# Layer 1's gathers moved into layer 2's first stage, which adds, normalises, turns and projects by quarters

## The chip, the cores and the metric

One Trainium2 chip, one core of it. The metric is the device time of one launch in microseconds, the median of the runs shown. A core has five engines that run side by side: TensorE (PE, matmuls and transposes), VectorE (DVE), ScalarE (ACT), GpSimd (POOL) and SyncE (SP, which here only issues DMAs). Each runs its own instructions strictly in the order in which they are written; they wait for one another on semaphores.

## The reference, cut to what matters

Four layers, each an attention-like part and a feed-forward part around a residual `x` of 2048 tokens by 128 features in float32. The change lies between layer 1's feed-forward part (each token goes through one of 64 experts) and the projections that open layer 2's attention-like part:

```
# layer 1, feed-forward: every token by the matrix of its own expert
sel = argmax(softmax(xt @ gate_w.T + gate_b), -1);  order = argsort(sel)
ys  = ragged_dot(xt[order], expert_w, counts) + expert_b[sel[order]]
x   = x + gb * (ys put back into the order of the tokens)
# layer 2, attention: norm over the features, then three projections
h = layernorm(x) * (1 + ca) + sa
R, K, V = h @ Wr.T, h @ Wk.T, h @ Wv.T
# then a scan over the tokens on R, K, V (leaky cells that fire at 1), and from it attn_out
x1 = layernorm(h + attn_out @ Wo.T)
```

## The kernel before, in words

Tokens are held as 16 tiles of 128 (`NT = 16`), four tiles to a quarter (`NC4 = 4` quarters of 512 tokens). A stage opens a `Block`, in which each engine has its own list; at the end of a block all engines meet before the next one begins, and at the end of a part of a layer they meet through a somewhat longer clean-up. What SP is told outside a block (the loads of a layer part) it issues when it gets there, while other engines may already be in the next block.

Layer 1's experts (`stage_l1_experts`): POOL scatters the normalised tokens by 16 indirect DMAs into a table in DRAM, sorted by expert in groups of 64 (L1856). SP reads it back in six loads (L1843), PE turns and multiplies (L1891, L1907), DVE multiplies by the gate into `y` (L1938), SP stores `y` in six pieces into a second table `sorted_out` (L1849). POOL waits for all six stores, then gathers each token's row back by 16 indirect DMAs into `back` (L1860), four to a quarter. For each quarter DVE waits for its four gathers, adds `back` to the residual `g.x` (L1945) and takes the statistics of its four tiles with `bn_stats` (L139). There the layer part ends.

Layer 2 (`layer2_spiking`) first has SP load its weights (L89: `l2_wrkvo`, `l2_ln1cols` and nine more, then L209), and ACT wait for `l2_ln1cols`. Then `stage_l2_mix`:

- DVE: `norm.start` (16 `bn_aggr`, L239, variance, L241; ACT's root, L419; reciprocal and one correction step, L243 to L248), `norm.normalise` of all 16 tiles (L403), then every second copy of projections out of PSUM (L2152), a fill with 0.9 (L2154), and the scan `lif` (L2049, L2050, then L2037 and L2040 in turn, 32 steps), on DVE alone.
- PE: six idle products to keep busy (L376), transposes of a quarter (L411), the three projections of a quarter (L2113, twelve in all), turning one quarter ahead of the one it projects.
- ACT: the root, for each quarter scale and shift out of PSUM into `hT` (L423), and the other half of the copies (L2131).
- POOL: waits for all 16 normalised tiles, then `RowsFinish` (six small operations in a chain, L225 to L231, which finish layer 2's rows of gates and scales), then two operations over all 2048 tokens that make `h_tm` (L2138 and L2141), needed only after the scan.

Two things are the same before and after: the order of DVE's scan, and everything after it.

Of the kernel before, what the change touches and what calls it, by code (L numbers as in the profile page):

```python
# [23 lines left out]
P = 128  # L24
# [354 lines left out]
class Norm:  # L379
# [1422 lines left out]
def stage_l1_experts(nc, d, g, loads, W, sorted_in, sorted_out, zeroed, weights_loaded, slot, member, gang_expert):  # L1802
# [6 lines left out]
    with Stage(nc, "l1exp") as st:  # L1809
        ident16 = loads["ident16"]  # L1810
# [4 lines left out]
        back = st.sb("back", [P, NT, P])  # L1815
# [17 lines left out]
        gathered = [st.sem(f"gathered{j}") for j in range(NC4)]  # L1833
        chain = st.sem("chain")
        with st.block() as block:

            @block.sync
            def _(sp):
                sp.wait_ge(scattered, 16 * NT)
                n = pairs // LOADS  # L1840
                for i in range(LOADS):
                    src = sorted_in[i * n * P:(i + 1) * n * P, :]
                    sp.dma_start(rows[:, i * n:(i + 1) * n, :], src.rearrange("(k p) f -> p k f", p=P))\  # L1843
                      .then_inc(rows_loaded[i], 16)
                for i in range(STORES):
                    sp.wait_ge(y_gated, QUADS // STORES * (i + 1))
                    m = GANGS // STORES
                    dst = sorted_out[i * m * GANG:(i + 1) * m * GANG, :]
                    sp.dma_start(dst.rearrange("(k p) f -> p k f", p=GANG), y[:, i * m:(i + 1) * m, :])\  # L1849
                      .then_inc(y_stored, 16)  # L1850

            @block.gpsimd
            def _(pool):
                pool.wait_ge(zeroed, 17)
                for t in range(NT):
                    pool.indirect_dma_start(out=sorted_in, out_offset=bass.IndirectOffsetOnAxis(  # L1856
                        ap=slot[:, t:t + 1], axis=0), in_=g.xn[:, t, :], in_offset=None).then_inc(scattered, 16)
                pool.wait_ge(y_stored, 16 * STORES)
                for t in range(NT):
                    pool.indirect_dma_start(out=back[:, t, :], out_offset=None, in_=sorted_out,  # L1860
                                            in_offset=bass.IndirectOffsetOnAxis(ap=slot[:, t:t + 1], axis=0))\
                        .then_inc(gathered[t // 4], 16)
                for j in range(NC4):
                    pool.wait_ge(gathered[j], 16 * 4)
# [62 lines left out]
            def _(dve):  # L1927
# [12 lines left out]
                link = Chain(dve, chain)  # L1940
                dve.wait_ge(bias_added, NC4)
                for j in range(NC4):
                    dve.wait_ge(gathered[j], 16 * 4)
                    ts = slice(4 * j, 4 * j + 4)
                    link(dve.tensor_tensor(g.x[:, ts, :], g.x[:, ts, :], back[:, ts, :], ALU.add))  # L1945
                    tile_stats(dve, g, g.x, range(4 * j, 4 * j + 4))


def layer1_experts(nc, d, g):
    sorted_in = nc.dram_tensor("l1_sorted_in", [GANGS * GANG, P], F32, kind="Internal").ap()  # L1950
    sorted_out = nc.dram_tensor("l1_sorted_out", [GANGS * GANG, P], F32, kind="Internal").ap()
# [124 lines left out]
def stage_l2_mix(nc, loads, g, h_tm, r):  # L2076

    with Stage(nc, "l2mix") as st:
        norm = adaln_norm(st, g, 2, SCALE_A, SHIFT_A)
        rows_finish = RowsFinish(st, 2)  # L2080
        g.rows_finished.add(2)
# [13 lines left out]
        out_done = st.sem("out_done")  # L2095
        chain = st.sem("chain")
        with st.block() as block:  # L2097

            @block.tensor
            def _(pe):  # L2100
                pe.wait_ge(loads.done, loads.all)
                norm.turn(pe, 0, ps_t[:, 0, :])
                for n in range(3 * NC4):
                    j, i = n // 3, n % 3
                    if i == 0:
                        if j + 1 < NC4:
                            if j >= 1:
                                norm.turned(pe, j - 1)
# [13 lines left out]
            def _(act):  # L2122
                norm.root(act)
                norm.scale(act, 0, ps_t[:, 0, :])
# [10 lines left out]
            def _(pool):  # L2135
                pool.wait_ge(norm.tile_normed, NT)
                rows_finish(pool, g)
# [8 lines left out]
            def _(dve):  # L2146
                link = Chain(dve, chain)
                norm.start(dve)
                norm.normalise(dve, range(NT))
                for n in range(1, 3 * NC4, 2):  # L2150
                    dve.wait_ge(in_done, n + 1)
                    dve.tensor_scalar(tokens_of(X_steps, LENGTH, n % 3, n // 3), by_chunk(ps[:, n % 6, :], LENGTH),  # L2152
                                      0.5, None, ALU.mult).then_inc(copied[1], 1)
# [1354 lines left out]
def program(nc, d, out, stages=None):  # L3508

    with ExitStack() as ctx:  # L3510
# [11 lines left out]
        g.stats = sb("stats", [P, NT, 6])  # L3522
        g.silu = sb("silu", [P, 4])
# [123 lines left out]
```

## Time and profile before

| | us |
|---|---|
| median of 3 runs | 1733.46 (1730.65 to 1736.72) |
| the profiled execution, its own time | 1726.0 |
| its span in the trace | 1724.2 |
| DVE busy over the span | 1303.6 (76%) |
| PE busy over the span | 1239.0 (72%) |
| last `y` gated to first gather started | 1016.06 to 1021.67 |
| 16 gathers, first start to last start | 1021.67 to 1040.50 |
| last add of layer 1 begins | 1042.99 |
| first instruction of DVE in layer 2 begins | 1045.63 |
| first scan instruction of DVE begins | 1066.68 |

Times with a decimal point and four digits before it are positions in the span of the profiled execution. The rows further down come from four views of it: the list of waits (which engine sat idle before which instruction, and what released it), the timeline (instructions in order of time, neighbours of one kind merged), the tile view (one buffer), and the table of stretches (busy time of each engine, granted clock of TensorE as a share of 2.4 GHz, and DMA). A matmul on float32 data is two passes in the trace and is counted x2.

### The profile page before, as it was taken

What the parts mean: (1) busy time and instruction counts of PE and PEld (TensorE: products, weight loads), DVE (VectorE), ACT (ScalarE), POOL (GpSimd) and SP (SyncE); (2) the same over time, 40 slices, a digit from 0 to 9 for tenths busy, and PEclk for the clock granted to TensorE, in tenths of its full rate; (3) what the DMA queues carried; (4) which work ended last, traced back from release to release, by engine and by line L of the source; (5) the groups of instructions that cost most, each with busy time, mean ns of one, the idle gap of its engine ahead of it and who ended that gap; (6) DMA issues with size and microseconds to landing.
All of it is one profiled execution on the core that took longest, in us unless ns stands there. A gap on an engine that the chain in (4) does not pass through costs nothing. (4 is left out here: it accounts for less than half of the span.)

```text
span 1724.2 us, 29793 instructions
## 1 busy us (share of the span) xinstructions
PE 1239.0 (72%) x10670; PEld 619.8 (36%) x10674; DVE 1303.6 (76%) x3511; ACT 889.7 (52%) x1757; POOL 236.1 (14%) x275
## 2 busy tenths in 40 slices
PE   7799999999999997574993453060215989824686
PEld 3122222222222223354982342040113547623445
DVE  6999999999999972447237236989897568578873
ACT  4099999999999996412521122020002775502553
POOL 2000000000000000003410324030003321000223
PEclk9599999999999999667995586565656988965668
DMA  2100000011000000000004331000001721031001
GB/s 73 37 14 27 21 21 21 22 28 28 23 21 20 21 2 2 15 29 1 1 1 188 101 84 46 0 0 1 1 0 27 228 68 43 4 116 49 22 22 31
DMA packets 45030, 62.88 MB, mean 36 GB/s; under 512 B 12785, under 2 KB 34356, under 8 KB 44484
## 3 DMA queue, kind: packets, MB, share of 16 engines
q1 hardware_dynamic: 38243, 49.71, 9.7%
q0 software_dynamic: 5440, 10.67, 2.3%
q8 instruction: 85, 1.39, 0.3%
q10 hardware_dynamic: 1200, 0.59, 0.1%
q14 instruction: 62, 0.51, 0.1%
HBM read 34.10 MB, written 13.63 MB: 28 GB/s over the span
## 5 line engine op out<-in xcount | busy, mean ns | idle before, releaser
L842 ACT ACTIVATE l0att_probs<-l0att_ps_sv 128x512 f32<-128x512 f32 x960 | 521.2, 596 | 80.0 <-PE l0att_ps_sv L811 68.1
L888 DVE TENSOR_REDUCE l0att_half_negmax<-l0att_ps_m 128x1 f32<-128x1024 f32 x480 | 547.1, 1216 | 5.6 <-PE l0att_ps_m L741 5.6
L773 PE MATMUL l0att_ps_sv<-l0att_probs,l_V_aug 128*32 128x256 f32 x4096 | 325.3, 392 | 4.8 <-ACT l0att_pv_sb L833 4.7
L811 PE MATMUL l0att_ps_sv<-l_Q,l_K 51*128 51x512 bf16 x992 | 194.5, 388 | 4.0 <-ACT l0att_probs L850 2.4
L741 PE MATMUL l0att_ps_m<-l_K,l_Q 48*128 48x512 bf16 x960 | 185.9, 384 | 11.1 <-DVE l0att_half_negmax L888 7.1
L773 PEld LDWEIGHTS l0att_ps_sv<-l0att_probs,l_V_aug 128*32 128x32 f32 x4096 | 83.0, 108 | 197.4 <-issue 100.9
L811 PEld LDWEIGHTS l0att_ps_sv<-l_Q,l_K 51*128 51x128 bf16 x992 | 48.0, 92 | 207.4 <-ACT l0att_probs L842 188.1
L472 POOL CAST l0att_nm<-l0att_negmax 128x16 bf16<-128x16 f32 x16 | 3.2, 198 | 515.0 <-DVE l0att_negmax L864 515.0
L2862 ACT ACTIVATE l3loc_probs<-l3loc_ps_s 128x320 f32<-128x320 f32 x128 | 48.9, 435 | 36.0 <-PE l3loc_ps_s L2839 35.3
L2040 DVE SCALAR_TENSOR_TENSOR l2spk_lif_v<-l2spk_U 128x64 f32<-128x64 f32 (+1 forms) x368 | 60.8, 207 | 0.0
L741 PEld LDWEIGHTS l0att_ps_m<-l_K,l_Q 48*128 48x128 bf16 x960 | 47.1, 95 | 28.5 <-DVE l0att_half_negmax L888 19.0
L2890 DVE TENSOR_REDUCE l3loc_negmax<-l3loc_ps_m 128x2 f32<-128x320 f32 x128 | 53.5, 484 | 3.8 <-PE l3loc_ps_m L2795 3.8
L2305 PE MATMUL l2spk_ps<-l_X,l2spk_w_terms 128*128 128x512 bf16 x48 | 11.8, 411 | 61.3 <-DVE l_X L2335 61.3
L2117 PE MATMUL l2mix_ps<-l_mix_l_wrkvo,l2mix_X 128*128 128x128 f32 x32 | 8.3, 441 | 65.4 <-DVE l2mix_X L2177 65.4
L3285 ACT ACTIVATE l3exp_passed<-l3f_experts_l_places,l3exp_neg_rank 128x257 bf16<-128x257 f32 x112 | 46.0, 500 | 0.0
L1938 DVE TENSOR_TENSOR l1exp_y<-l1exp_ps_y,mod_rows 64x512 f32<-64x512 f32 x24 | 16.4, 683 | 36.3 <-PE l1exp_ps_y L1907 36.3
L1562 DVE TENSOR_TENSOR l1chunk_T<-l1chunk_T,l1chunk_ps_t 128x512 f32<-128x512 f32 x20 | 13.8, 688 | 36.0 <-PE l1chunk_ps_t L1463 36.0
L2223 ACT ACTIVATE l2hid_half_b<-l_hidden_l_b 128x4 f32<-128x4 f32 x1 | 0.2, 205 | 75.5 <-PEq L2097 75.5
L2325 ACT ACTIVATE l2spk_U<-l2spk_ps,l2spk_half_b 128x512 f32<-128x512 f32 x2 | 2.3, 1127 | 70.8 <-PE l2spk_ps L2305 70.7
L1517 POOL TENSOR_TENSOR l1chunk_C<-l1chunk_A,l_chunks_masks 128x2048 f32<-128x2048 f32 x7 | 31.7, 4534 | 47.3 <-DVE l1chunk_A L1549 25.9
L2037 DVE SCALAR_TENSOR_TENSOR l2spk_U<-l2spk_lif_v,l_X 128x64 f32<-128x64 f32 x212 | 37.5, 219 | 0.4 <-DVE l2spk_lif_mid L2055 0.4
L3243 PE MATMUL l3exp_ps_c<-l3exp_part,l3exp_ones 128*128 128x15 bf16 x56 | 10.7, 191 | 36.1 <-DVE l3exp_part L3392 36.0
(736 smaller groups left out, 2391.8 us busy)
## 6 DMA issues: line engine op xcount, KB each, us to landing
l_K<-l_kp SPq DMA_DIRECT2D x192, 32.0 KB
l_Q<-l_qp SPq DMA_DIRECT2D x192, 32.0 KB
l1ffn_W<-in_l_expert_w_dram SPq DMA_DIRECT2D x1, 4096.0 KB
l3f_experts_l_w<-in_l_w_dram SPq DMA_DIRECT2D x2, 2048.0 KB
l_sorted_in<-l1ffn_zeros SPq DMA_DIRECT2D x1, 3072.0 KB
l1exp_rows<-l_sorted_in SPq DMA_DIRECT2D x6, 512.0 KB, 5.6
l_sorted_out<-l1exp_y SPq DMA_DIRECT2D x6, 512.0 KB, 4.6
l_Q<-in_local_mask_q_dram POOLq DMA_DIRECT2D x2, 1170.0 KB, 17.3
```

Source lines behind the costliest of these rows:

```text
L741: mm = pe.matmul(dst[:, i * BANK:(i + 1) * BANK], Q[at, h % HEAD_BUFS, c1(t)], K[at, h % HEAD_BUFS, c4(2 * half + i)], start=True, stop=True)
L773: mm = pe.matmul(ps_v[32 * c:32 * c + 32, cols], V_aug[:, kt, h, :], probs[:, kt % 2, c, cols], start=(kt == 0 and part == 0), stop=(kt == ...
L811: pe.matmul(dst, K[at, h % HEAD_BUFS, c1(kt)], Q[at, h % HEAD_BUFS, c4(2 * pair + i)], start=True, stop=True).then_inc(last_scored[i] if l ...
L842: act.activation(probs[:, kt % 2, c, :], ps_s[:, n % 3, :], ACT.Exp).then_inc(expd, 1)
L888: dve.tensor_reduce(half_negmax[:, h % 2, t, half:half + 1], src, AX_X, ALU.max, negate=True).then_inc(m_read, 1)
L1517: pool.tensor_tensor(C[:, l % 2, :, :], A[:], mask(l, NT), ALU.mult).then_inc(c_ready, 1)
L1938: dve.tensor_tensor(y[:, 4 * n:4 * n + 4, :], ps_y[0:GANG, n % 4, :].rearrange("p (k f) -> p k f", k=4), gates, ALU.mult).then_inc(y_gated, 1)
L2037: link.mark(dve.scalar_tensor_tensor(U[:, t, half], before[:, half], 0.5, X[:, t, half], ALU.mult, ALU.add))
L2040: link.mark(dve.scalar_tensor_tensor(v[:, half], U[:, t, half], 1.0, U[:, t, half], ALU.is_lt, ALU.mult))
L2862: act.activation(probs[:, n % 3, 2 * half:2 * half + 2, :].rearrange("p h c -> p (h c)"), ps_s[:, u % SCORE_BUFS, 0:2 * SPAN], ACT.Exp).th ...
L2890: dve.tensor_reduce(negmax[:, 2 * half:2 * half + 2, t], heads2(src[:, 0:2 * SPAN]), AX_X, ALU.max, negate=True).then_inc(m_read, 1)
L3285: ins = act.activation(passed[:, e % 2, t, :], place_row[:], ACT.Sign, bias=neg_rank[:, e, t:t + 1])
```

## The change

The 16 gathers leave layer 1's last stage and open layer 2's first stage on POOL; SP waits for the six stores before layer 1's stage ends. `RowsFinish` of layer 2 moves from POOL's list in layer 2 to POOL's list in layer 1, behind the scatters. The index tile `slot` is kept over both layers. DVE's add and statistics move to layer 2, and everything that it does up to the projections' copies is done one quarter at a time, with the copies that are its own between the quarters. PE no longer turns one quarter ahead, and runs twelve idle products ahead of the turns of quarters 1 to 3. ACT takes the root by quarters.

```
     # class Norm
+    def start_quarter(self, dve, link, j):
+        ts = slice(4 * j, 4 * j + 4)
+        mv, var, std, rstd, corr = (buf[:, ts] for buf in (self.mv, self.var, self.std, self.rstd, self.corr))
+        for t in range(4 * j, 4 * j + 4):
+            link.mark(dve.bn_stats(self.g.stats[:, t, :], self.src[:, t, :]))
+        link.wait()
+        for t in range(4 * j, 4 * j + 4):
+            link.mark(dve.bn_aggr(self.mv[:, t, :], self.g.stats[:, t, :]))
+        link.wait()
+        dve.tensor_scalar(var, mv[:, :, 1], LN_EPS, None, ALU.add).then_inc(self.var_ready, 1)
+        dve.wait_ge(self.std_ready, j + 1)
+        link(dve.reciprocal(rstd, std))
+        link(dve.tensor_tensor(corr, rstd, rstd, ALU.mult))
+        link(dve.tensor_tensor(corr, corr, var, ALU.mult))
+        link(dve.tensor_scalar(corr, corr, -0.5, 1.5, ALU.mult, ALU.add))
+        link(dve.tensor_tensor(rstd, rstd, corr, ALU.mult))
+    def root_quarter(self, act, j):
+        ts = slice(4 * j, 4 * j + 4)
+        act.wait_ge(self.var_ready, j + 1)
+        act.activation(self.std[:, ts], self.var[:, ts], ACT.Sqrt).then_inc(self.std_ready, 1)
...
     # stage_l1_experts, SP, POOL, DVE
+                sp.wait_ge(y_stored, 16 * STORES)
...
-                pool.wait_ge(y_stored, 16 * STORES)
-                for t in range(NT):
-                    pool.indirect_dma_start(out=back[:, t, :], out_offset=None, in_=sorted_out, ...)\
-                        .then_inc(gathered[t // 4], 16)
-                for j in range(NC4):
-                    pool.wait_ge(gathered[j], 16 * 4)
+                pool.wait_ge(scattered, 16 * NT)
+                rows_finish(pool, g)
...
-                for j in range(NC4):
-                    dve.wait_ge(gathered[j], 16 * 4)
-                    ts = slice(4 * j, 4 * j + 4)
-                    link(dve.tensor_tensor(g.x[:, ts, :], g.x[:, ts, :], back[:, ts, :], ALU.add))
-                    tile_stats(dve, g, g.x, range(4 * j, 4 * j + 4))
...
     # stage_l2_mix, PE
-                norm.turn(pe, 0, ps_t[:, 0, :])
...
                     if i == 0:
-                        if j + 1 < NC4:
-                            if j >= 1:
-                                norm.turned(pe, j - 1)
-                            norm.turn(pe, j + 1, ps_t[:, (j + 1) % 2, :])
+                        if j >= 1:
+                            keep_busy(pe, g, ps_t[:, j % 2, :], 12)
+                        norm.turn(pe, j, ps_t[:, j % 2, :])
                         norm.turned(pe, j)
...
     # stage_l2_mix, ACT
-                    if i == 0 and j + 1 < NC4:
-                        norm.scale(act, j + 1, ps_t[:, (j + 1) % 2, :])
+                    if i == 0:
+                        norm.root_quarter(act, j)
+                        norm.scale(act, j, ps_t[:, j % 2, :])
...
     # stage_l2_mix, POOL
+                for t in range(NT):
+                    pool.indirect_dma_start(out=back[:, t, :], out_offset=None, in_=g.sorted_out, ...)\
+                        .then_inc(gathered[t // 4], 16)
                 pool.wait_ge(norm.tile_normed, NT)
-                rows_finish(pool, g)
...
     # stage_l2_mix, DVE
-                norm.start(dve)
-                norm.normalise(dve, range(NT))
-                for n in range(1, 3 * NC4, 2):
-                    dve.wait_ge(in_done, n + 1)
-                    dve.tensor_scalar(tokens_of(X_steps, LENGTH, n % 3, n // 3), ..., 0.5, None, ALU.mult)...
+                for j in range(NC4):
+                    ts = slice(4 * j, 4 * j + 4)
+                    dve.wait_ge(gathered[j], 16 * 4)
+                    link(dve.tensor_tensor(g.x[:, ts, :], g.x[:, ts, :], back[:, ts, :], ALU.add))
+                    norm.start_quarter(dve, link, j)
+                    norm.normalise(dve, range(4 * j, 4 * j + 4))
+                    for n in range(3 * j, 3 * j + 3):
+                        if n % 2 == 1:
+                            dve.wait_ge(in_done, n + 1)
+                            dve.tensor_scalar(tokens_of(X_steps, LENGTH, n % 3, j), ..., 0.5, None, ALU.mult)...
```

## Rows read from the trace of the kernel before

**Rows 1.** Waits, 1008 to 1085: who waited for what, total us, times, longest.

```profile
POOL l1exp_back L1860 <- DMA l_sorted_out<-l1exp_y: 46.8, 1, 46.8
DVE x_res L1945 <- DMA l1exp_back<-l_sorted_out,l1ffn_slot: 21.3, 4, 11.3
DVE l2mix_X L2152 <- PE l2mix_ps L2113: 5.3, 6, 1.1
DVE l2mix_norm_rstd L243 <- ACT l2mix_norm_std L419: 1.9, 1, 1.9
```

**Rows 2.** Timeline, end of layer 1: start us, us, engine, line, op.

```profile
1016.06 0.68 DVE L1938 TENSOR_TENSOR l1exp_y<-l1exp_ps_y,mod_rows 64x512 f32<-64x512 f32 x1 [0.19 <-PE l1exp_ps_y L1907]
1021.67 0.99 POOL L1860 DMA_INDIRECT l1exp_back<-l_sorted_out,l1ffn_slot  x1 [46.79 <-DMA l_sorted_out<-l1exp_y]
1028.08 0.69 DVE L1945 TENSOR_TENSOR x_res<-x_res,l1exp_back 128x512 f32<-128x512 f32 x1 [11.33 <-DMA l1exp_back<-l_sorted_out,l1ffn_slot]
1028.81 0.87 DVE L139 BATCH_NORM_STATS2 stats<-x_res 128x6 f32<-128x128 f32 x4
...
1040.50 0.94 POOL L1860 DMA_INDIRECT l1exp_back<-l_sorted_out,l1ffn_slot  x1 [0.31 <-issue]
...
1043.71 0.87 DVE L139 BATCH_NORM_STATS2 stats<-x_res 128x6 f32<-128x128 f32 x4
```

**Rows 3.** Timeline, from layer 2's first instruction to the scan.

```profile
1045.63 1.17 DVE L239 BATCH_NORM_AGGREGATE l2mix_norm_mv<-stats 128x2 f32<-128x6 f32 x16 [1.05 <-PEq L3532]
...
1048.36 2.93 PE L376 MATMUL l2mix_ps_t<-ident_sb 128*128 128x128 f32 x12 [32.34 <-DMA l_mix_l_wrkvo<-in_l_wrkvo_dram]
...
1050.06 4.19 DVE L403 TENSOR_SCALAR xn<-x_res,l2mix_norm_mv,l2mix_norm_rstd 128x128 f32<-128x128 f32 x16
...
1054.34 0.87 POOL L225 TENSOR_SCALAR mod_rows<-mod_rows 128x256 f32<-128x256 f32 x1 [12.90 <-DVE xn L403]
...
1059.85 4.54 POOL L2138 TENSOR_TENSOR l_h_tm<-xn,mod_rows 128x2048 f32<-128x2048 f32 x1
...
1064.47 4.50 POOL L2141 TENSOR_TENSOR l_h_tm<-l_h_tm,mod_rows 128x2048 f32<-128x2048 f32 x1
1064.78 1.03 DVE L2152 TENSOR_SCALAR l2mix_X<-l2mix_ps 128x512 f32<-128x512 f32 x1 [0.67 <-PE l2mix_ps L2113]
...
1066.68 2.58 DVE L2037 SCALAR_TENSOR_TENSOR l2mix_U<-l2mix_lif_shifted,l2mix_X 128x96 f32<-128x96 f32 x2
1069.18 0.42 DVE L2040 SCALAR_TENSOR_TENSOR l2mix_lif_v<-l2mix_U 128x96 f32<-128x96 f32 x2
```

**Rows 4.** Timeline, start of the experts' stage: the first indirect DMA of a block.

```profile
954.03 0.28 DVE L1930 TENSOR_TENSOR l1exp_gated_table<-l1ffn_bias_l_expert_b,mod_rows 64x128 f32<-64x128 f32 x1 [0.38 <-PEq L1744]
954.74 1.13 POOL L1856 DMA_INDIRECT l_sorted_in<-xn,l1ffn_slot  x1 [13.81 <-POOLq L1744]
```

**Rows 5.** Timeline, layer 2's next stage, the same norm and first projections.

```profile
1141.66 0.17 DVE L241 TENSOR_SCALAR l2hid_norm_var<-l2hid_norm_mv 128x16 f32<-128x16 f32 x1
...
1143.25 4.19 DVE L403 TENSOR_SCALAR l_h_tm<-l_x_tm,l2hid_norm_mv,l2hid_norm_rstd 128x128 f32<-128x128 f32 x16
...
1145.76 3.70 PE L2218 MATMUL l2hid_ps<-hT,l_hidden_l_w1T 128*128 128x512 f32 x8
...
1147.87 1.11 DVE L2244 TENSOR_SCALAR l_X<-l2hid_ps,l2hid_half_b 128x512 f32<-128x512 f32 x1 [0.42 <-PE l2hid_ps L2218]
```

**Rows 6.** Stretches: us, busy (instructions) of PE, PEld, DVE, ACT, POOL; clock, DMA share, GB/s.

```profile
1018.00:1020.00 2.00, 0.00 (x0) 0.00 (x0) 0.00 (x0) 0.00 (x0) 0.00 (x0) 0.87 0.82 175
1050.00:1052.00 2.00, 2.00 (x12) 2.00 (x11) 1.96 (x9) 0.00 (x0) 0.00 (x0) 0.50 0.81 203
...
1053.00:1054.00 1.00, 0.99 (x2) 0.68 (x3) 1.00 (x5) 0.78 (x1) 0.00 (x0) 0.69 0.42 166
1054.00:1055.00 1.00, 1.00 (x3) 0.40 (x3) 0.25 (x1) 0.54 (x1) 0.66 (x1) 1.00 0.00 0
```

**Rows 7.** Stretches in layer 3's experts, same columns: TensorE about 70% busy with gaps.

```profile
1610.00:1612.00 2.00, 1.64 (x13) 1.23 (x13) 1.65 (x9) 1.06 (x3) 0.00 (x0) 1.00 0.00 0
...
1614.00:1616.00 2.00, 1.72 (x10) 1.57 (x9) 1.77 (x10) 0.18 (x1) 1.20 (x2) 0.50 0.33 90
```

**Rows 8.** Tile views of layer 1's gathers and, below, layer 3's: 16 each.

```profile
DMA to landing us min/median/max: 2.4/2.5/2.7
...
DMA to landing us min/median/max: 2.2/2.8/3.7
```

More of the change, by code:

```diff
@@ L1809, in stage_l1_experts @@
     with Stage(nc, "l1exp") as st:
+        rows_finish = RowsFinish(st, 2)
+        g.rows_finished.add(2)
         ident16 = loads["ident16"]
@@ L1814, in stage_l1_experts @@
         y = st.sb("y", [GANG, GANGS, P])
-        back = st.sb("back", [P, NT, P])
         chosen = st.sb("chosen", [EXPERTS, S])
@@ L1832, in stage_l1_experts @@
         y_stored = st.sem("y_stored")
-        gathered = [st.sem(f"gathered{j}") for j in range(NC4)]
-        chain = st.sem("chain")
         with st.block() as block:
@@ L1857, in _ @@
                         ap=slot[:, t:t + 1], axis=0), in_=g.xn[:, t, :], in_offset=None).then_inc(scattered, 16)
-                pool.wait_ge(y_stored, 16 * STORES)
-                for t in range(NT):
-                    pool.indirect_dma_start(out=back[:, t, :], out_offset=None, in_=sorted_out,
-                                            in_offset=bass.IndirectOffsetOnAxis(ap=slot[:, t:t + 1], axis=0))\
-                        .then_inc(gathered[t // 4], 16)
-                for j in range(NC4):
-                    pool.wait_ge(gathered[j], 16 * 4)
+                pool.wait_ge(scattered, 16 * NT)
+                rows_finish(pool, g)
             @block.tensor
@@ L1939, in _ @@
                         "p (k f) -> p k f", k=4), gates, ALU.mult).then_inc(y_gated, 1)
-                link = Chain(dve, chain)
                 dve.wait_ge(bias_added, NC4)
-                for j in range(NC4):
-                    dve.wait_ge(gathered[j], 16 * 4)
-                    ts = slice(4 * j, 4 * j + 4)
-                    link(dve.tensor_tensor(g.x[:, ts, :], g.x[:, ts, :], back[:, ts, :], ALU.add))
-                    tile_stats(dve, g, g.x, range(4 * j, 4 * j + 4))
 def layer1_experts(nc, d, g):
@@ L1951, in layer1_experts @@
     sorted_out = nc.dram_tensor("l1_sorted_out", [GANGS * GANG, P], F32, kind="Internal").ap()
+    slot = g.slot
+    g.sorted_out = sorted_out
     ZEROS = 8
@@ L1955, in layer1_experts @@
         zeros = st.sb("zeros", [P, ZEROS * P])
-        slot = st.sb("slot", [P, NT], I32)
         idx = st.sb("idx", [P, NT, 8], U32)
@@ L2079, in stage_l2_mix @@
         norm = adaln_norm(st, g, 2, SCALE_A, SHIFT_A)
-        rows_finish = RowsFinish(st, 2)
-        g.rows_finished.add(2)
         w = loads["l2_wrkvo"]
@@ L2095, in stage_l2_mix @@
         out_done = st.sem("out_done")
+        back = st.sb("back", [P, NT, P])
+        gathered = [st.sem(f"gathered{j}") for j in range(NC4)]
         chain = st.sem("chain")
@@ L2122, in _ @@
             def _(act):
-                norm.root(act)
-                norm.scale(act, 0, ps_t[:, 0, :])
                 for n in range(3 * NC4):
                     j, i = n // 3, n % 3
-                    if i == 0 and j + 1 < NC4:
-                        norm.scale(act, j + 1, ps_t[:, (j + 1) % 2, :])
+                    if i == 0:
+                        norm.root_quarter(act, j)
+                        norm.scale(act, j, ps_t[:, j % 2, :])
                     if n % 2 == 0:
@@ L2135, in _ @@
             def _(pool):
+                for t in range(NT):
+                    pool.indirect_dma_start(out=back[:, t, :], out_offset=None, in_=g.sorted_out,
+                                            in_offset=bass.IndirectOffsetOnAxis(ap=g.slot[:, t:t + 1], axis=0))\
+                        .then_inc(gathered[t // 4], 16)
                 pool.wait_ge(norm.tile_normed, NT)
-                rows_finish(pool, g)
                 pool.tensor_tensor(h_tm[:], g.xn[:], bcast(mod_row(g, 2, SCALE_A).unsqueeze(1), P, NT, P),
@@ L2147, in _ @@
                 link = Chain(dve, chain)
-                norm.start(dve)
-                norm.normalise(dve, range(NT))
-                for n in range(1, 3 * NC4, 2):
-                    dve.wait_ge(in_done, n + 1)
-                    dve.tensor_scalar(tokens_of(X_steps, LENGTH, n % 3, n // 3), by_chunk(ps[:, n % 6, :], LENGTH),
-                                      0.5, None, ALU.mult).then_inc(copied[1], 1)
+                for j in range(NC4):
[7 more added lines that the diff above has]
+                            dve.wait_ge(in_done, n + 1)
+                            dve.tensor_scalar(tokens_of(X_steps, LENGTH, n % 3, j), by_chunk(ps[:, n % 6, :], LENGTH),
+                                              0.5, None, ALU.mult).then_inc(copied[1], 1)
                 link.mark(dve.memset(decay[:], 0.9))
@@ L3522, in program @@
         g.stats = sb("stats", [P, NT, 6])
+        g.slot = sb("slot", [P, NT], I32)
         g.silu = sb("silu", [P, 4])
```

## Prediction

> **What bounds the kernel now.** I read the waits around the change first, then the timeline. In the waits [rows 1] the reader is to see that between layer 1's last product and layer 2's scan nobody computes much: DVE sits 21.3 us before its four adds, waiting for gathers. The timeline [rows 2] gives the order: last `y` gated at 1016.06, the stores landed at the latest at 1021.67, when POOL begins, and then 16 gathers at one per (1040.50 - 1021.67) / 15 = 1.255 us, so a quarter each 5.02 us. From then on the path is: last gather, add and statistics, change of stage (1044.58 to 1045.63, 1.05 us), norm, 16 normalised tiles (1050.06 to 1054.25), twelve projections, copies until 1065.81, scan [rows 3]. The scan is on DVE alone and everything behind it is unchanged, so the question is when it gets going.
>
> That moment isn't 1066.68, where its first instruction starts. The first pair takes 2.58 us where the next takes 0.42, and it ends at 1069.26, just behind POOL's second `h_tm` operation, which ends at 1068.97 [rows 3]. DVE's copies out of PSUM beside the same operation took their normal 1.03. So the scan's first instruction, which reads two tensors of SBUF, stood still until POOL was through. I therefore count from the end of POOL: 1068.97 before.
>
> The Trainium skill (SBUF — State Buffer, section "SBUF: two separate sides") says that VectorE and GpSimd share one pair of ports, that it is an exclusive lock for a whole instruction, and that a VectorE instruction with two SBUF inputs needs it against a GpSimd instruction that reads SBUF. By this rule the start of the scan follows POOL's end after the change too; the trace's 2.58 against 0.42 us agrees.
>
> **What the change does, part by part.** Call A the start of the first add (1028.08 before) and T the end of the last normalised tile (1054.25 before).
>
> *The gathers' start.* It now lies behind a change of layer part. The stores still land by 1021.67, then 1.05 us as at 1044.58 to 1045.63 [rows 2, 3]; the first indirect DMA of a block starts 0.71 us behind DVE's first instruction there and takes 1.13 instead of 0.95 [rows 4]. Sum 1.9; the landing may be some 0.2 earlier than 1021.67, so I take 1.7. The ends are 1.05 (no start-up) and 1.9. Besides, SP now issues layer 2's twelve loads in the same microseconds as the first gathers; before they filled 0.81 of the DMA engines at 203 GB/s with nobody in need of them but PE and ACT [rows 6]. The trace has no gather under such a load; the nearest are layer 3's, 2.2 to 3.7 us to landing against 2.4 to 2.7 here [rows 8]. Ends 0 and 1.2, I take 0.8, since most of the load stands in the first quarter's way. A = 1028.08 + 2.5 = 1030.6.
>
> *A quarter's front on DVE.* Add and statistics 1.60 (1028.08 to 1029.68) [rows 2]. Four aggregates: 16 take 1.17, at about 0.07 apart and 0.15 the last, so 0.35 plus 0.05 of waits [rows 3]. Variance, ACT's root, reciprocal and correction: 1141.66 to 1143.25, 1.59, which hardly depends on width since these are a chain of short operations with waits [rows 5]; the narrower 4 columns could save 0.1 in all. Four normalised tiles: 16 in 4.19, so 1.11. Sum 4.7. Before, the norm's chain was paid once for 16 tiles; now four times, 3 x 1.59 = 4.8 us more of DVE. The 1.9 us in which DVE waited for ACT, held by the load of `l2_ln1cols` [rows 1], goes: that load now lands before A.
>
> *A quarter's back.* This is the heart of it. DVE's copy of quarter j stands in its list ahead of the add of quarter j+1, and waits for PE, which waits for ACT, which waits for PE's turns of that very quarter. Queued behind the waiting copy: the next quarter's add, and through it everything. What that costs is in the next stage, which has the same turns and projections: fourth tile normalised at 1143.25 + 1.11 = 1144.36, first projection at 1145.76, DVE's copy of the second at 1147.87, so 3.51 from tile to copy [rows 5]. With 1.05 of the copy [rows 3] and a wait, 4.6 us for quarters 0 and 2, which have one copy of DVE (n = 1, 7). Quarters 1 and 3 have two (n = 3, 5 and 9, 11); the later one waits for one projection more. Eight passes take 3.70, a projection 0.86 to 0.92: 3.51 + 0.86 + 1.05 = 5.45.
>
> So a quarter occupies DVE for 9.3 or 10.15 us, twice the 5.02 at which quarters land: from quarter 1 on the gathers are hidden and DVE's chain is the bound. T = A + 4 x 4.7 + 4.6 + 5.45 + 4.6 = A + 33.45, at TensorE's upper clock.
>
> *The clock.* The granted clock was 0.50 when the stage began, and 1.00 from 1054 on, after TensorE had worked without a pause since 1048.36; it fell to 0.50 within 4 us of TensorE's last work at the end of layer 1 [rows 3, 6]. In the changed stage the six idle products run as soon as `l2_wrkvo` is there (2.73 us after the stage begins, as at 1045.63 to 1048.36, so about 1025.4, to 1028.3), TensorE then idles until the turns at about 1034, and quarter 0's first two projections run at 1.2 GHz: 2 x 0.86 = 1.7 more. Then projections and twelve idle products run without a break, which should raise it. Later quarters have TensorE about 65% busy in pieces; in layer 3 at such a share the clock was 1.00 in one stretch and 0.50 two stretches on [rows 7]. A later single-copy quarter at the lower level costs 1.7, a double-copy one 2.6; what quarter 3 loses is behind T, hidden by POOL (below). Ends 0 and 4.3 for quarters 1 and 2; I take 1.0, since twelve idle products stand just ahead. The idle products themselves (24 passes, 2.6 us; at the lower clock 5.9 by the 2.93 for 12 [rows 3]) lie beside DVE's copy and front, 4.9 us up to the next quarter's first tile; at the upper clock they cost nothing, at the lower one up to 2.3 a quarter.
>
> T = 1030.6 + 33.45 + 1.7 + 1.0 = 1066.75.
>
> *POOL.* `RowsFinish` (1054.34 to 1059.85, 5.5 us [rows 3]) goes from between T and `h_tm` to the time behind the scatters, when POOL has nothing to do and DVE waits for the first product: free. POOL then needs 4.54 + 4.50 + 0.2 = 9.2 behind T. DVE's last copies end at T + 5.45, fills at T + 6.3, so the scan again stands until POOL's end, T + 9.2 = 1075.95. Against 1068.97: **+7.0 us**. Moving `RowsFinish` away gives 5.5 us of this path back; without it the sum would be +12.5.
>
> *Further places.* SP's wait for the stores replaces POOL's and adds nothing. The index tile and the semaphores cost nothing on the path. Behind the scan all is as before.
>
> The profiled execution's own time was 1726.0 (span 1724.2); with +7.0 it is 1733.0. The median of the runs lies 7.5 above it, so I forecast 1733.46 + 7.0 = 1740.5.
>
> **Rivals.**
>
> 1. *Less: TensorE is at the upper clock soon and the gathers start early.* A = 1029.1 (only the 1.05), no cold quarter: T = 1062.6, POOL's end 1071.8, +2.8; or POOL does not hold the scan, then the first pair ends at about T + 6.7, also near +4. For it: the low ends of each term, and the idle products. Against it: TensorE's pause of about 6 us (1028.3 to 1034.5) ahead of quarter 0. Time about 1736.5, within 0.3%.
>
> 2. *More: each quarter begins at the lower clock.* 1.7 + 2.6 + 1.7 instead of 2.7, and the idle products, twice as long, delay the turns of two quarters by 1 to 2 us: +10.5 to +14. For it: the alternation in layer 3 [rows 7], and before each quarter's turns TensorE has paused 1.5 to 2.5 us. Against it: projections and idle products make over 5 us in a row. Time about 1745.
>
> 3. *Faster: the quarters do overlap.* If DVE's wait for its copies is short enough that a quarter takes no more than the 5.02 us at which it lands, the last quarter's add is ready at 1042.99 + 2.5, T = 1050.2, and POOL's end 1059.4: -9.6, 1724. It decides where DVE's period per quarter falls under 5 us; break-even (T = 1059.8) is a period of (1059.8 - 1030.6 - 4.7) / 3 = 8.2 us. Against it: front and back as measured add to 9.3 and 10.15, and DVE's list has no way around the copy. Only if both parts are a fifth shorter than in these rows does it begin to gain.
>
> 4. *It does what it says but the time is elsewhere*: the sum rests on POOL and DVE at one place; nothing in the trace suggests another path there.
>
> **How the numbers follow.** About 0.3% (5.2 us) is what a measurement of this kernel can tell from no change. Forecast +5.2 to +10: chance 0.42. Rival 1 (0 to +5.2): 0.30. Rival 2 (beyond +10): 0.18. Rival 3 and other gains: 0.10, of which 0.02 is a gain under 0.3%. Slower: 0.42 + 0.18 = 0.60; same: 0.32; faster: 0.08. The range leaves out the gains and the far end of rival 2: from -1 to +15, 1732.5 to 1748.5. The likeliest case's own range is 1738.5 to 1743.5.
>
> **What would show it.** Right: DVE's adds about 9.5 to 12 us apart, with waits of about 2.5 us for `l2mix_ps` before each quarter's first copy of DVE, and no wait for gathers after the first; first add at 1030 to 1031; the scan's first pair again ending with POOL's second `h_tm` operation, near 1076; clock 0.50 in quarter 0. Wrong: adds 5 us apart (rival 3); the first pair of the scan at 0.42 us; gathers waited for more than once; a clock at 0.50 throughout (rival 2) or never after 1035 (rival 1).

## The result, and the profile after

| | median us | runs | ratio to before, 95% interval |
|---|---|---|---|
| before | 1729.90 | 20 | |
| after | 1737.45 | 20 | 1.0047 [1.0035, 1.0060] |

The change makes the kernel slower by 7.55 us. The forecast was 1740.5: 3 us too high, because it started from the median of three runs, 1733.46, where that of all twenty is 1729.90; the step of +7.0 that it put on top was right. In the profiled executions the span went from 1724.2 to 1734.0.

The span is a poor measure of the place: with nothing changed there, layer 3's local attention began 13.6 us later in the second trace and the last step of its expert search 10.5, while the scan had ended 6.9 later. I use one inside the trace, called **D** below: from the end of the last gated `y` of layer 1 to the end of the scan's first pair on DVE. Before it is 1069.26 - 1016.74 = 52.5 [rows 2, 3]; after, 1076.60 - 1017.01 = 59.6. The difference is +7.1 us; forecast were +7.0, and the medians differ by 7.55.

The changed kernel from the last gated `y` to the scan (timeline, DVE's and POOL's lines that answer to [rows 2, 3]):

```profile
1016.33 0.68 DVE L1955 TENSOR_TENSOR l1exp_y<-l1exp_ps_y,mod_rows 64x512 f32<-64x512 f32 x1 [0.19 <-PE l1exp_ps_y L1924]
...
1023.52 1.08 POOL L2146 DMA_INDIRECT l2mix_back<-l_sorted_out,slot  x1 [41.04 <-POOLq L3550]
...
1027.45 0.95 POOL L2146 DMA_INDIRECT l2mix_back<-l_sorted_out,slot  x1 [0.30 <-issue]
...
1031.41 0.69 DVE L2163 TENSOR_TENSOR x_res<-x_res,l2mix_back 128x512 f32<-128x512 f32 x1 [14.40 <-DMA l2mix_back<-l_sorted_out,slot]
...
1034.91 1.12 DVE L425 TENSOR_SCALAR xn<-x_res,l2mix_norm_mv,l2mix_norm_rstd 128x128 f32<-128x128 f32 x4
...
1041.37 1.02 DVE L2169 TENSOR_SCALAR l2mix_X<-l2mix_ps 128x512 f32<-128x512 f32 x1 [5.34 <-PE l2mix_ps L2123]
1042.24 0.67 DVE L2163 TENSOR_TENSOR x_res<-x_res,l2mix_back 128x512 f32<-128x512 f32 x1
1042.43 1.29 POOL L2146 DMA_INDIRECT l2mix_back<-l_sorted_out,slot  x1 [0.30 <-issue]
...
1049.25 1.03 DVE L2169 TENSOR_SCALAR l2mix_X<-l2mix_ps 128x512 f32<-128x512 f32 x1 [2.42 <-PE l2mix_ps L2123]
...
1051.86 0.67 DVE L2163 TENSOR_TENSOR x_res<-x_res,l2mix_back 128x512 f32<-128x512 f32 x1
...
1061.67 1.03 DVE L2169 TENSOR_SCALAR l2mix_X<-l2mix_ps 128x512 f32<-128x512 f32 x1 [5.22 <-PE l2mix_ps L2123]
1062.54 0.67 DVE L2163 TENSOR_TENSOR x_res<-x_res,l2mix_back 128x512 f32<-128x512 f32 x1
...
1066.02 1.12 DVE L425 TENSOR_SCALAR xn<-x_res,l2mix_norm_mv,l2mix_norm_rstd 128x128 f32<-128x128 f32 x4
...
1071.82 4.50 POOL L2153 TENSOR_TENSOR l_h_tm<-l_h_tm,mod_rows 128x2048 f32<-128x2048 f32 x1
...
1073.17 3.43 DVE L2049 SCALAR_TENSOR_TENSOR l2mix_U<-l2mix_lif_shifted,l2mix_X 128x96 f32<-128x96 f32 x2
```

The reader is to see three things. The adds (L2163) begin at 1031.41, 1042.24, 1051.86 and 1062.54, so 10.8, 9.6 and 10.7 us apart, while POOL issues a quarter's gathers in 5.0. Only the first add waits for a gather; what precedes each later one is a copy (L2169) that waited for PE. And the scan's first pair ends with POOL's second `h_tm` operation, as before [rows 3]. The waits of this stretch say the same in two lines: DVE's wait for gathers fell from 21.3 us in four to 14.4 in one, its wait for projections rose from 5.3 to 16.7 [rows 1].

```profile
DVE l2mix_X L2169 <- PE l2mix_ps L2123: 16.7, 6, 5.3
DVE x_res L2163 <- DMA l2mix_back<-l_sorted_out,slot: 14.4, 1, 14.4
```

TensorE's clock in the same trace, in the columns of [rows 6], one stretch ahead of quarter 0 and one in each quarter's projections or their start:

```profile
1029.00:1031.00 2.00, 0.00 (x0) 0.00 (x0) 0.00 (x0) 0.00 (x0) 1.59 (x2) 0.96 0.85 224
...
1036.00:1038.00 2.00, 1.13 (x4) 0.73 (x4) 0.03 (x1) 0.78 (x1) 1.50 (x2) 0.50 0.23 55
1048.00:1050.00 2.00, 1.92 (x5) 0.96 (x6) 0.75 (x1) 0.03 (x1) 0.00 (x0) 1.00 0.00 0
1058.00:1060.00 2.00, 2.00 (x3) 0.97 (x4) 0.00 (x0) 0.04 (x1) 0.00 (x0) 0.50 0.00 0
1068.00:1070.00 2.00, 1.61 (x4) 0.87 (x5) 0.45 (x1) 0.33 (x1) 2.00 (x1) 1.00 0.00 0
```

Quarters 0 and 2 projected at 0.50 (1.2 GHz), 1 and 3 at 1.00 (2.4 GHz). DVE waited 5.34 and 5.22 us for its first copy in the former and 2.42 in the latter. Only part of that is the clock: in quarters 0 and 2 DVE's first copy is of the quarter's second projection, in 1 and 3 of its first. At the upper clock the wait in quarters 0 and 2 is 3.31 and 3.27 (e5 below), so the clock's share is 2.0 us each.

### The profile page after: what moved, and what is told of

Read it like the earlier page. It is cut to its first block and busy times, and to the rows that moved or that the text cites. A ratio compares the mean times of both kernels' runs of the same rounds, so it can differ in the third digit from the quotient of the medians.

```text
span 1734.0 us, 29959 instructions
## 1 busy us (share of the span) xinstructions
PE 1260.9 (73%) x10746; PEld 630.2 (36%) x10746; DVE 1307.4 (75%) x3529; ACT 891.1 (51%) x1760; POOL 235.8 (14%) x275
## 5 line engine op out<-in xcount | busy, mean ns | idle before, releaser
L3260 PE MATMUL l3exp_ps_c<-l3exp_part,l3exp_ones 128*128 128x15 bf16 x56 | 10.7, 191 | 37.7 <-DVE l3exp_part L3409 37.6
```

## The experiments

All twelve, with D and what the theory gave for it. Ratios are to the kernel before, on the same chip in the same hour. Each difference of D from the kernel before lies inside the interval of its ratio, so D stands for what the whole kernel gains or loses, as far as the intervals can tell.

| | D forecast | D measured | ratio, 95% interval |
|---|---|---|---|
| before | | 52.5 | 1 |
| after | | 59.6 | 1.0047 [1.0035, 1.0060] |
| e1 gathers moved, nothing by quarters | 49.6 | 50.0 | 0.9995 [0.9977, 1.0013] |
| e2 before, `RowsFinish` early | 50.4 | 50.7 | 0.9986 [0.9973, 0.9999] |
| e3 copies one quarter later, no idle products | 46.7 | 46.3 | 0.9978 [0.9963, 0.9994] |
| e4 `h_tm` by quarters | 56.6 | 61.2 | 1.0047 [1.0030, 1.0064] |
| e5 more idle products | 56.2 | 57.3 | 1.0018 [1.0006, 1.0029] |
| e6 other loads late | 58.2 | 59.4 | 1.0029 [1.0016, 1.0042] |
| e7 = e3 and e4 | 45.4 | 46.9 | 0.9972 [0.9959, 0.9985] |
| e8 = e3 and e6 | 44.9 | 44.0 | 0.9949 [0.9934, 0.9964] |
| e9 `RowsFinish` back in layer 2 | 65.1 | 60.6 (65.2, see there) | 1.0070 [1.0046, 1.0094] |
| e10 no idle products | 62.2 | 62.2 | 1.0060 [1.0037, 1.0082] |
| e11 = e3 with idle products | 49.7 | 48.8 | 0.9977 [0.9960, 0.9993] |
| e12 the changed kernel again | 57 to 62 | 58.9 | 1.0056 [1.0036, 1.0075] |

**e1: is it the move or the quarters?** Against the changed kernel:

```
-                    norm.start_quarter(dve, link, j)
-                    norm.normalise(dve, range(4 * j, 4 * j + 4))
-                    for n in range(3 * j, 3 * j + 3): ...copies
+                    for t in range(4 * j, 4 * j + 4): ...bn_stats
+                norm.start(dve); norm.normalise(dve, range(NT)); copies
     # and TensorE and ScalarE as in the kernel before
```

> The changed kernel with the gathers, the adds and RowsFinish where the change puts them, but with the norm, the turns, the projections and the copies again as before: all four adds first, then one norm over 16 tiles, TensorE turning one quarter ahead, no idle products ahead of quarters 1 to 3. Measure: from the end of the last gated y of layer 1 to the end of the scan's first pair, 52.5 us in the kernel before (1016.74 to 1069.26), 59.6 in the changed one (1017.01 to 1076.60). Theory (the loss is VectorE's list, in which a quarter's copies stand ahead of the next quarter's add): the adds come every 5 us, the last about 28 us behind the last gated y, the norm's last tile at 36.7, RowsFinish is out of the way, the pair ends at about 49.6: 2.9 us less than before and 10 less than the changed kernel. Rival (the loss is the gathers' later start and their company by the loads, and the quartering is neutral): about 59, as the changed kernel.

Timeline of DVE and POOL, the last add to the scan:

```profile
1043.85 0.69 DVE L2166 TENSOR_TENSOR x_res<-x_res,l2mix_back 128x512 f32<-128x512 f32 x1 [3.33 <-DMA l2mix_back<-l_sorted_out,slot]
1048.27 4.19 DVE L425 TENSOR_SCALAR xn<-x_res,l2mix_norm_mv,l2mix_norm_rstd 128x128 f32<-128x128 f32 x16
...
1057.15 4.54 POOL L2156 TENSOR_TENSOR l_h_tm<-l_h_tm,mod_rows 128x2048 f32<-128x2048 f32 x1
...
1065.47 0.43 DVE L2049 SCALAR_TENSOR_TENSOR l2mix_U<-l2mix_lif_shifted,l2mix_X 128x96 f32<-128x96 f32 x2
```

The last add begins 27.9 us behind the last gated `y` instead of 45.5; D is 50.0, 9.6 less than in the changed kernel with the same gathers at the same place. So the move costs nothing, and the quarters cost all of it. The gathers do come later: the last add begins 27.9 us behind the last gated `y` where it was 26.3 before. But the change of stage, 1.05 us, no longer stands behind it, and DVE's wait for ACT's root fell from 1.92 to 0.28. Against the kernel before D is 2.5 less, and most of that is `RowsFinish`, which is early in e1 as well: e2, which has nothing but that, comes to 50.7. The ratio, 0.05% down with 0.18% either way, holds this gain and no change too.

**e2: what holds the scan.** In the kernel before, `rows_finish` goes from POOL's list in layer 2 to just behind the scatters.

> The kernel before with RowsFinish alone moved behind the scatters. Measure as in the first experiment (52.5 us before). Theory (POOL's h_tm holds the scan's first pair): POOL's second operation ends at about 1063.5, before the scan starts at 1066.7, the pair takes 0.42 instead of 2.58 us, and the measure is 50.4, 2.1 us less. Rival (the first pair is slow in itself, or held by something else): the pair still takes 2.6 us and the measure stays at 52.5.

```profile
1060.08 4.54 POOL L2142 TENSOR_TENSOR l_h_tm<-l_h_tm,mod_rows 128x2048 f32<-128x2048 f32 x1
...
1067.49 0.43 DVE L2041 SCALAR_TENSOR_TENSOR l2mix_U<-l2mix_lif_shifted,l2mix_X 128x96 f32<-128x96 f32 x2
```

POOL ends at 1064.62, the pair begins at 1067.49 and takes 0.43. With POOL out of the way the same instruction isn't slow. That piece of the change is a gain by itself, 1.8 us in D, and its interval lies below 1, if barely.

**e3 and e11: the order on DVE.**

```
                     norm.normalise(dve, range(4 * j, 4 * j + 4))
-                    for n in range(3 * j, 3 * j + 3): ...copies of quarter j
+                    if j >= 1:
+                        copies(j - 1)
+                copies(NC4 - 1)
     # ScalarE: root of quarter j + 1 right behind the scale of quarter j
     # TensorE, in e3 alone:
-                        if j >= 1:
-                            keep_busy(pe, g, ps_t[:, j % 2, :], 12)
```

> The changed kernel with VectorE's copies of quarter j written behind the add and norm of quarter j+1, ScalarE's root of quarter j+1 ahead of its copies of quarter j, and no idle products ahead of quarters 1 to 3. Measure as in the first experiment (59.6 us in the changed kernel). Theory (VectorE's wait for its copies is the loss): adds 4.7 to 7 us apart instead of 9.6 to 10.8, last normalised tile about 37 us behind the last gated y, measure 46.7: 13 less than the changed kernel, 6 less than before. Rival (the period is the engines' work, not the order, with ScalarE or TensorE the next bound): adds 8 us or more apart, measure 55 or more.

> The third experiment with the twelve idle products left ahead of quarters 1 to 3: VectorE's copies one quarter later, ScalarE's root earlier, nothing else against the changed kernel. Measure as in the first experiment (46.3 us in the third, 59.6 in the changed kernel). Theory: the order of the copies alone is worth nearly all of it; with VectorE no longer waiting, the idle products, 2.84 us each time, now stand ahead of turns that are ready: TensorE becomes the bound at about 7.5 us a quarter, measure 49.7, 3.4 more than the third, 9.9 less than the changed kernel. Rival (the gain of the third came from leaving the idle products out): near 59.

The scan's first pair in e3, then DVE's waits of e3 and of e11, from the last gated `y` to the scan:

```profile
1060.07 3.44 DVE L2049 SCALAR_TENSOR_TENSOR l2mix_U<-l2mix_lif_shifted,l2mix_X 128x96 f32<-128x96 f32 x2
```

```profile
DVE l2mix_X L2164 <- PE l2mix_ps L2121: 2.9, 3, 1.5
```

```profile
DVE l2mix_X L2166 <- PE l2mix_ps L2123: 6.2, 3, 4.8
DVE l2mix_norm_rstd L412 <- ACT l2mix_norm_std L421: 3.8, 4, 2.6
```

The wait for projections is 2.9 us where it was 16.7; D fell by 13.3. With the idle products left in (e11) it still fell by 10.8: four fifths of the gain is order alone, that of DVE's list together with ACT's earlier root. The other 2.5 us are those products, which here stand ahead of turns that are ready. On the whole kernel e3 and e11 can't be told apart.

**e4 and e7: `h_tm` by quarters.** POOL's two operations over 16 tiles become eight over four, each pair behind its own quarter's normalised tiles.

> The changed kernel with POOL's two h_tm operations done quarter by quarter as the quarters are normalised, instead of over all 16 tiles at the end. Measure as in the first experiment (59.6 us in the changed kernel). Theory (the scan is held only until POOL is through): POOL ends about 2.4 us behind the last normalised tile, the first pair takes 0.42 instead of 3.43 us, measure 56.6, 3.0 less. Rival (POOL's operations now stand in the way of VectorE's add and normalise of the next quarter, up to 1.15 us each): 1.8 less or nothing.

> The third and fourth experiment together: VectorE's copies one quarter later, and h_tm by quarters on POOL. Measure as in the first experiment (46.3 in the third, in which the scan's first pair took 3.44 us). The fourth showed that POOL's smaller operations hold single operations of VectorE's front for 0.6 to 0.7 us each, 1.3 in the second quarter. Theory: the pair takes 0.43, saving 3.0, and the fronts of quarters 2 and 3 lose 1.3 and 0.8: measure 45.4. Rival (the fronts, now without pauses between them, lose more, or TensorE's clock falls): 47 or more.

Both missed. The scan's pair did take 0.43 in both. But the small operations stood in the way of the fronts, and in e4 the clock fell as well. Of e4, one held operation of quarter 1's front and the clock in that quarter's projections:

```profile
1044.65 0.79 DVE L410 TENSOR_SCALAR l2mix_norm_var<-l2mix_norm_mv 128x4 f32<-128x4 f32 x1
```

```profile
1050.00:1052.00 2.00, 2.00 (x3) 0.96 (x4) 0.00 (x0) 0.00 (x0) 1.26 (x1) 0.50 0.00 0
```

The holds cost e4 only 1.3 us (this operation, and one of 0.16 that took 0.84). The larger part of its miss is the clock: quarter 1's projections took 5.27 us instead of 2.84, and with the holds the adds on either side of them lie 13.5 us apart instead of 9.6; quarter 3's took 4.35 instead of 2.84, with POOL no longer there to hide it. Both quarters ran at 1.00 in the changed kernel. Timeline of e7, POOL's and DVE's lines of quarter 2:

```profile
1048.08 1.37 DVE L413 TENSOR_TENSOR l2mix_norm_corr<-l2mix_norm_rstd 128x4 f32<-128x4 f32 x1
1048.13 1.28 POOL L2152 TENSOR_TENSOR l_h_tm<-xn,mod_rows 128x512 f32<-128x512 f32 x1
...
1049.49 1.28 POOL L2155 TENSOR_TENSOR l_h_tm<-l_h_tm,mod_rows 128x512 f32<-128x512 f32 x1
1049.67 1.13 DVE L415 TENSOR_SCALAR l2mix_norm_corr<-l2mix_norm_corr 128x4 f32<-128x4 f32 x1
1050.84 0.16 DVE L416 TENSOR_TENSOR l2mix_norm_rstd<-l2mix_norm_rstd,l2mix_norm_corr 128x4 f32<-128x4 f32 x1
1050.85 1.27 POOL L2152 TENSOR_TENSOR l_h_tm<-xn,mod_rows 128x512 f32<-128x512 f32 x1
1051.04 3.03 DVE L425 TENSOR_SCALAR xn<-x_res,l2mix_norm_mv,l2mix_norm_rstd 128x128 f32<-128x128 f32 x4
```

Operations that take 0.16 and 0.17 without POOL take 1.37 and 1.13, and four normalised tiles 3.03 instead of 1.12. I had allowed 1.3 us for that quarter; it was about 4.

**e5 and e10: idle products.** e5 runs 30 instead of 6 ahead of quarter 0 and 20 instead of 12 ahead of quarter 2; e10 leaves out the 12 ahead of quarters 1 to 3.

> The changed kernel with more idle products on TensorE: 30 instead of 6 ahead of quarter 0, and 20 instead of 12 ahead of quarter 2; nothing else. Measure as in the first experiment (59.6 us in the changed kernel, where quarters 0 and 2 projected at 1.2 GHz and VectorE waited 5.3 and 5.2 us for its copy, against 2.4 in quarters 1 and 3). Theory (the lower clock costs two single projections' time in each of two quarters): granted clock 1.00 from quarter 0's turns on, waits of 3.5 or less, measure 56.2, 3.4 less. Rival (the idle products run into the turns and delay them, or the clock falls all the same): 59 or more.

> The changed kernel without the twelve idle products ahead of quarters 1 to 3; the six ahead of quarter 0 stay. Measure as in the first experiment (59.6 us in the changed kernel, clock low in quarters 0 and 2, high in 1 and 3). Theory (they are what lifts the clock for a following quarter): the clock is 0.50 in all four quarters, VectorE waits about 5.3 us for the first copy of each and longer for the second, measure 62.2, 2.6 more. Rival (the projections lift it alone, or the idle products do harm): 59.6 or less.

Stretches of e5 in its four quarters, then of e10, in the columns of [rows 6]:

```profile
1036.00:1040.00 4.00, 1.92 (x9) 0.96 (x8) 1.92 (x9) 0.78 (x1) 3.09 (x4) 1.00 0.21 55
1048.00:1050.00 2.00, 1.87 (x3) 0.85 (x4) 0.00 (x0) 0.08 (x1) 0.00 (x0) 0.58 0.00 0
1056.00:1060.00 4.00, 2.79 (x17) 1.81 (x16) 1.95 (x9) 0.81 (x2) 0.00 (x0) 1.00 0.01 2
1068.00:1070.00 2.00, 1.80 (x3) 0.90 (x4) 0.24 (x1) 0.15 (x1) 2.00 (x1) 0.70 0.00 0
```

```profile
1036.00:1038.00 2.00, 1.13 (x3) 0.65 (x4) 0.00 (x0) 0.78 (x1) 1.66 (x2) 0.50 0.23 64
1048.00:1050.00 2.00, 2.00 (x3) 0.97 (x4) 0.00 (x0) 0.00 (x0) 0.00 (x0) 0.50 0.00 0
1058.00:1060.00 2.00, 1.24 (x4) 0.72 (x4) 0.92 (x4) 0.52 (x1) 0.00 (x0) 0.50 0.01 4
1070.00:1072.00 2.00, 1.13 (x2) 0.50 (x2) 0.00 (x0) 0.78 (x1) 2.00 (x1) 0.50 0.00 0
```

In e5 quarters 0 and 2 ran at 1.00 and their waits fell to 3.31 and 3.27, as forecast; but now quarters 1 and 3, untouched, slipped to the lower level for part of their projections (4.54 us each instead of 2.84). Quarters 0 and 2 gained 3.9 us, quarter 1 gave 1.7 of them back, and quarter 3's loss is hidden behind POOL: D fell by 2.3 instead of 3.4. Both theory and rival hold in part. In e10 all four quarters began at 0.50, and D rose by the 2.6 forecast. So the products are worth their place in the changed kernel, and the lower level in quarters 0 and 2 costs it 2.0 us each (5.34 against 3.31, 5.22 against 3.27).

**e6 and e8: the loads beside the gathers.** SP issues all of layer 2's loads but `l2_wrkvo` and `l2_ln1cols` behind the last gather; e8 does it in e3.

```
+            @block.sync
+            def _(sp):
+                sp.wait_ge(gathered[NC4 - 1], 16 * 4)
+                issue_late(sp)
```

> The changed kernel with layer 2's loads other than l2_wrkvo and l2_ln1cols issued by SP only after the last gather has landed. Measure as in the first experiment (59.6 us in the changed kernel); the first add begins 14.4 us behind the last gated y there, its fourth gather 10.4. Theory (the loads beside the gathers hold up the first quarter's landing): fourth gather to first add 2.6 instead of 4.0 us, first add at 13.0, measure 58.2. Rival (the late landing is the new place of the gathers, not the loads): first add at 14.4 and 59.6. Should the clock come out otherwise in one of the quarters, the first add alone decides.

> The third experiment with the loads of the sixth: VectorE's copies one quarter later, and layer 2's other loads issued after the last gather has landed. Measure as in the first experiment (46.3 in the third). Theory (the first quarter's landing starts a chain without slack): first add at 13.4 instead of 14.8, measure 44.9, and the loads still land far ahead of layer 2's next stage. Rival (the later quarters are bound by their own gathers, every 5 us): first add at 13.4, measure unchanged at 46.3.

In e6 the fourth gather was issued at 1027.23 and the first add began at 1029.80 (2.57 us, 13.0 behind the last gated `y`), against 3.96 and 14.4 in the changed kernel. So the 1.4 us are the loads': the ten traces with the loads beside the gathers have 3.5 to 4.4 us from that issue to the first add, the two with the loads put later 2.5 and 2.6. D hardly moved all the same, because quarter 1 met the lower clock this time and took 11.3 us from add to add instead of 9.6. In e8 the gain went through: the first add came 1.9 us earlier than in e3 (12.97 against 14.83), and D fell by 2.3. e8 from the first add on, DVE's lines and POOL's last:

```profile
1034.60 0.69 DVE L2178 TENSOR_TENSOR x_res<-x_res,l2mix_back 128x512 f32<-128x512 f32 x1 [12.97 <-DMA l2mix_back<-l_sorted_out,slot]
...
1039.66 0.69 DVE L2178 TENSOR_TENSOR x_res<-x_res,l2mix_back 128x512 f32<-128x512 f32 x1 [0.32 <-DMA l2mix_back<-l_sorted_out,slot]
...
1045.31 0.68 DVE L2178 TENSOR_TENSOR x_res<-x_res,l2mix_back 128x512 f32<-128x512 f32 x1
...
1051.56 0.69 DVE L2178 TENSOR_TENSOR x_res<-x_res,l2mix_back 128x512 f32<-128x512 f32 x1
...
1060.84 4.51 POOL L2161 TENSOR_TENSOR l_h_tm<-l_h_tm,mod_rows 128x2048 f32<-128x2048 f32 x1
...
1063.89 1.74 DVE L2052 SCALAR_TENSOR_TENSOR l2mix_U<-l2mix_lif_shifted,l2mix_X 128x96 f32<-128x96 f32 x2
```

The adds are 5.1, 5.7 and 6.3 us apart, near the gathers' own 5.0. This kernel beats both the kernel before and the changed one: 1723.45 against 1732.42 us for the kernel before, 0.51% less, and D 8.5 less.

**e9: `RowsFinish` where it was.**

> The changed kernel with RowsFinish of layer 2 put back where it was, on POOL between the last normalised tile and h_tm. Measure as in the first experiment (59.6 us in the changed kernel). Theory (POOL's end starts the scan): the six operations of 5.5 us come on top, the scan's first pair takes about 8.9 us, measure 65.1, which is 12.6 above the kernel before. Rival (the scan's wait has another cause): 59.6. The clock of a quarter may move either by up to 2.6; the distance from the last normalised tile to the pair's end, 9.5 us in the changed kernel, doesn't depend on it: 15.0 by the theory.

```profile
1073.14 4.50 POOL L2150 TENSOR_TENSOR l_h_tm<-xn,mod_rows 128x2048 f32<-128x2048 f32 x1
1073.59 4.33 DVE L2046 SCALAR_TENSOR_TENSOR l2mix_U<-l2mix_lif_shifted,l2mix_X 128x96 f32<-128x96 f32 x2
1077.72 4.55 POOL L2153 TENSOR_TENSOR l_h_tm<-l_h_tm,mod_rows 128x2048 f32<-128x2048 f32 x1
1077.84 4.71 DVE L2049 SCALAR_TENSOR_TENSOR l2mix_lif_v<-l2mix_U 128x96 f32<-128x96 f32 x2
```

D as I had defined it missed: 60.6. The scan now started during POOL's first operation, which held its first instruction for 4.16 us; the second took its normal 0.24, and the third was held again, by POOL's second operation. Counted to the end of that second hold, 1082.55 - 1017.32 = 65.2, against 65.1. The ratio fits the long count better: 1.0070 is 12.1 us more than the kernel before, where 65.2 says 12.7 and 60.6 says 8.1, the low end of the interval. So `RowsFinish` behind the scatters is worth 5.6 us in the changed kernel, by a longer way than forecast.

**e12: a second trace of the changed kernel.**

> The changed kernel itself once more, for a second trace. Theory (the granted clock of a quarter depends on how its pauses fall): which quarters run at the lower clock may differ from the first trace (0 and 2), and with it the measure, by 1.7 or 2.6 us a quarter, so 57 to 62; quarter 0 is at 0.50 again, since TensorE pauses 6.7 us ahead of its turns. Rival (the clock is fixed by the program): quarters 0 and 2 again, 59.6 within 0.3.

The rival holds for the clock: quarters 0 and 2 again waited 5.29 and 5.07 us and quarters 1 and 3 2.41 and 2.42, and e9, whose quarters are those of the changed kernel, has 5.28, 5.22, 2.41 and 2.41. It doesn't hold for its 59.6 within 0.3: D is 58.9, 0.7 less than in the first trace, of which 0.5 is the first landing (first add at 13.9 instead of 14.4). In these three traces unchanged pauses left the levels as they were; in e4, e5 and e6, where pauses changed, the levels did too.

## Why the prediction was right, point by point

Times after are given less 0.27 us, by which layer 1's last gated `y` was later in the second trace.

- **The gathers' start**: forecast 1.7 later, measured 1023.52 - 1021.67 - 0.27 = 1.6. (The first gather began 6.5 us behind the last gated `y` in every trace of the new place; in the old place it was 4.9 in the trace before and 5.5 in e2.)
- **The loads' company**: forecast 0.8, at most 1.2; measured 1.4 in this trace, 0.9 to 1.8 over all ten that have it, and e6 took it away whole. This term was mis-sized, its range too: layer 3's gathers weren't near enough a case.
- **A quarter's front**: forecast 4.7, measured 4.6 each time.
- **A quarter's back at the upper clock**: with two copies 5.45 forecast, 5.0 measured (1046.82 to 1051.86); with one 4.6 forecast, 4.2 in e5. The next add begins before the copy's end.
- **The clock**: 2.7 forecast, 1.7 for quarter 0 and 1.0 for the rest. Measured against e5 it was 2.0 for quarter 0 and 2.0 for quarter 2, nothing for quarter 1: 4.0.
- **T**: 1066.75 forecast, 1067.14 - 0.27 = 1066.87 measured.
- **POOL to the scan**: 9.2 behind T forecast, 9.2 measured, and the scan held as before.
- **The signs**: adds 9.6 to 10.8 apart, one wait for gathers, the clock at 0.50 in quarter 0 and the pair ending with POOL at 1076.60 came as written. Two didn't: the first add began at 1031.14 (less the 0.27), just past 1030 to 1031, for the loads; and the "waits of about 2.5 us" before each quarter's first copy were 5.3 in quarters 0 and 2. That sign didn't fit the prediction's own sum either, which has 3.51 from tile to copy there at the upper clock.
- **Rival 1** (upper clock, early start) fell with quarter 0 and the loads; **rival 2** (every quarter at the lower clock) is what e10 does, without the idle products and so at +9.7 in D, just short of the rival's +10.5; in the changed kernel it was two quarters of four; **rival 3** (quarters overlap) is what e8 does once DVE's list allows it: 8.5 less in D, where the rival had said 9.6.

The sum's agreement to 0.1 us is partly luck: the loads' term was too small by 0.6 and the clock's by 1.3, the three backs too large by 1.2, the fronts and the start by 0.5. The mechanism, though, is shown from both sides: e1 takes the quarters away, e11 only the order, and each takes the whole loss away (D 50.0 and 48.8, below the 52.5 before).

What stays open: the last 0.5 us between D's +7.1 and the 7.55 of the medians is below what they can tell. The 52.5 is from one trace of the kernel before, and the landing of the stores alone differs by 0.5 us between that trace and e2's. And I can't say from the traces what decides whether a given pause costs the clock.

## What to carry to other kernels

Cutting a stage into pieces so that it can follow arriving data gains nothing while one engine's list holds, between two pieces, a wait for the end of the first piece's way through the other engines: compare the time of such a round trip with the interval at which data arrive, and write the piece's last step one piece later. An operation that is off the critical path can still end it if it holds something that the next critical instruction needs; look for a first instruction that takes many times what its followers do. Before loads are moved, see which transfer on the path they will meet.

## What the runs showed of the hardware

- GpSimd's operations on SBUF held VectorE's with two SBUF inputs, and in e7 also its normalise and its short `tensor_scalar`, until they were through: 3.43 us for a pair of 0.42, 1.37 for one of 0.16, 1.13 for one of 0.17; VectorE's copies out of PSUM beside the same kind of operation kept their 1.03. Where two such operations came in a row, one instruction of VectorE passed at its normal 0.24 us where one ended and the next began (e9). GpSimd was held too: in the changed kernel its issue of a gather that began inside an add of VectorE's (1042.43, the add from 1042.24 to 1042.91) took 1.29 us instead of 0.94. There are eight such issues of 1.01 us and more, in this trace and those of e6, e7, e8, e10, e11 and e12, and each ends 0.81 or 0.82 us behind the add. The Trainium skill (SBUF — State Buffer, section "SBUF: two separate sides") calls it an exclusive lock held for a whole instruction, with the loser fully blocked; the traces agree.
- The six idle products of the changed kernel ended at 1028.61, the granted clock rose to 1.00 at about 1029, with TensorE idle, and was at 0.50 again before the first turn at 1035.31. In e12 the same products raised nothing before quarter 0. So the six were of no use to quarter 0 in either trace. e5's 30 ended at 1036.28, 1.1 us ahead of the first turn, and there the clock was 1.00 through quarter 0's projections.
- Beside the loads, with 0.85 of the DMA engines busy at 224 GB/s (loads and gathers together), the add that waits for the fourth gather came 3.96 us behind its issue; with the loads put later, 2.57.
